# A spectral layer and an attention convolution on one core: the mode loads held behind the row transform, and one pair of transform 1 with 128 stationary columns

## The reference

```python
x = x + _L0_conv_ref(_gn(x), L0_conv_weight, L0_conv_fc_w, L0_conv_fc_b)
x = x + _L1_conv_ref(_gn(x), L1_conv_dft_weight, L1_conv_ksm_w, L1_conv_bias, L1_conv_fbm_scale)
```

```python
x_ft = jnp.fft.rfftn(x, axes=(-2, -1))
blk = jnp.einsum('bimn,hiomn->bhomn', x_ft[:, :, :m1, :m2], w_c)      # 32 x 32 modes
...
xr = jnp.fft.irfftn(out_ft, s=(H, W), axes=(-2, -1))
return jnp.einsum('bchw,oc->bohw', xr, fc_w) + fc_b[None, :, None, None]
```

## Time and profile before

| | |
|---|---|
| median of 3 runs | 139.55 us (138.25 to 139.67) |
| the profiled execution | 139.57 us, of it the span 137.8 us |
| busy: PE, DVE, ACT, POOL | 122.5, 87.8, 70.7, 52.8 us |
| TensorE's granted clock | 0.995 of full speed |
| code packets (queue 8) | 16, 0.26 MB |
| data moved | 25.17 MB, mean 183 GB/s |

### The profile page before, as it was taken

How to read it: one execution, slowest core, us unless ns; L and a number is a source line. 1 busy time by engine, 2 the same in 40 slices (tenths; PEclk the granted TensorE clock), 3 DMA queues, 4 the chain that set the end, 5 groups by cost and what they waited for, 6 DMA issues and landing times.

```text
span 137.8 us, 4822 instructions
## 1 busy us (share of the span) xinstructions
PE 122.5 (89%) x2060; PEld 91.8 (67%) x2060; DVE 87.8 (64%) x201; ACT 70.7 (51%) x143; POOL 52.8 (38%) x44
## 2 busy tenths in 40 slices
PE   0799997969997969979999979989999999999970
PEld 0799997869996959979999969873323432223230
DVE  0077696879996743553357685999873789922340
ACT  0468458538965336523317775644998329311100
POOL 7993000009999999999600550130500000000000
PEclk9999999999999999999999999999999999999997
DMA  3999999999500036787876899887989968884477
GB/s 90 268 272 257 233 222 357 302 384 399 204 5 7 0 81 156 171 203 165 181 164 153 172 178 153 180 202 164 168 184 175 211 156 189 195 191 105 104 162 143
DMA packets 71892, 25.17 MB, mean 183 GB/s; under 512 B 67904, under 2 KB 68160, under 8 KB 71872
## 3 DMA queue, kind: packets, MB, share of 16 engines
q1 hardware_dynamic: 70784, 24.62, 77.2%
q10 hardware_dynamic: 1088, 0.26, 0.9%
HBM read 14.38 MB, written 4.19 MB: 135 GB/s over the span
## 4 chain that ended last, share of the span: by engine, by line
PE 86%; issue 5%; DVE 3%; DMA 2%; ACT 0%; SPq 0%
PE slot L1050 27%; PE slot L882 14%; PE slot L963 11%; PE slot L978 8%; PE slot L941 6%; PE slot L952 5%; PE slot L908 3%; PE aggp L1008 3%; PE slot L904 3%; DMA x_buf<-x 2%; PE small L904 1%; PE aggp L904 1%; DVE kern L780 1%; PE aggp L941 1%; PE small L892 1%
## 5 line engine op out<-in xcount | busy, mean ns | idle before, releaser
L1050 PE MATMUL slot<-y_buf,conv_w 128*32 128x512 f32 (+1 forms) x136 | 31.7, 603 | 0.0
L1050 PE MATMUL slot<-w_buf,conv_w 128*32 128x512 f32 (+1 forms) x136 | 31.7, 603 | 0.0
L882 PE MATMUL slot<-cst,x_buf 128*64 128x64 f32 x512 | 19.0, 241 | 5.3 <-DMA x_buf<-x 4.5
L882 PEld LDWEIGHTS slot<-cst,x_buf 128*64 128x64 f32 x512 | 18.4, 154 | 5.6 <-issue 5.5
L821 DVE TENSOR_TENSOR bd_buf<-slot,q_buf 128x512 f32<-128x512 f32 (+1 forms) x17 | 11.0, 670 | 9.3 <-PE slot L1050 9.1
L1050 PEld LDWEIGHTS slot<-y_buf,conv_w 128*32 128x32 f32 x136 | 8.3, 109 | 12.6 <-issue 12.0
L441 POOL TENSOR_TENSOR x_buf<-y_buf 128x1024 f32<-128x1024 f32 x4 | 7.7, 1934 | 22.5 <-DVE y_buf L709 22.5
L978 PE MATMUL slot<-cst,t_buf 128*128 128x128 f32 x128 | 15.5, 278 | 0.8 <-issue 0.8
L978 PEld LDWEIGHTS slot<-cst,t_buf 128*128 128x128 f32 x128 | 14.7, 192 | 1.4 <-issue 1.2
L963 PE MATMUL slot<-cst,r_buf 128*64 128x128 f32 x256 | 14.6, 274 | 0.7 <-ACT r_buf L491 0.7
L613 DVE TENSOR_REDUCE row_sq<-q_buf 128x16 f32<-128x1024 f32 (+1 forms) x9 | 9.8, 1097 | 7.7 <-ACT q_buf L459 7.7
(11 more groups left out here) (128 smaller groups left out, 222.7 us busy)
## 6 DMA issues: line engine op xcount, KB each, us to landing
x_buf<-x SPq DMA_DIRECT2D x16, 256.0 KB, 4.3
w_buf<-w_modes SPq DMA_DIRECT2D x16, 256.0 KB, 5.0
x_buf<-x SPq DMA_DIRECT2D x32, 128.0 KB, 3.1
w_buf<-y_buf SPq DMA_DIRECT2D x16, 256.0 KB, 5.9
out<-bd_buf SPq DMA_DIRECT2D x28, 128.0 KB, 2.8
t_buf<-dft_w SPq DMA_DIRECT2D x4, 288.0 KB, 5.3
t_buf<-x_buf SPq DMA_DIRECT2D x8, 128.0 KB, 2.4
r_buf<-x_buf SPq DMA_DIRECT2D x8, 128.0 KB, 3.4
```

Of the source, the lines that this page charges most:

```text
L882: last = pe.matmul(ps[64 * ri:64 * ri + 64, col:col + 64], x_part(k)[:, i, q, :], const("fwd_h")[:, 64 * ri:64 * ri + 64], start=True, sto ...
L1050: last = pe.matmul(ps[32 * j:32 * j + 32, 32 * u0:32 * u1], cw[r][:, b, k, :], src, start=(k == terms[0][0]), stop=(k == terms[-1][0]))
```

## The change

There are two edits. SyncE waits until `f1_done` has reached 14 before it issues the first mode load. And in `f2_part` the pair (k, s) = (1, 3), that is images 6 and 7 of part 1 in both groups, takes the form with one matmul of 128 stationary columns for an image in place of two with 64; what is computed stays the same.

```diff
--- before.py
+++ after.py
@@ -318,6 +318,7 @@
                     load_rows(sp, k, q)
                 if k == 1:
                     sp.dma_start(cst[:, 128:EPS1 + 1], consts[:, 128:EPS1 + 1]).then_inc(fwd_w_in, 16)
+            sp.wait_ge(f1_done, 14)
             for ml in range(4):
                 for q in range(4):
                     sp.dma_start(modes[:, ml, 8 * q:8 * q + 8].rearrange("p n xo -> p (n xo)"), w_modes[ml, q]
@@ -900,7 +901,7 @@
                 ml = 4 * xx + k
                 for b in (2 * s, 2 * s + 1):
                     col, f = 64 * b, 4 * ml
-                    if k >= 2:
+                    if k >= 2 or (k, s) == (1, 3):
                         last = pe.matmul(ps[:, col:col + 64], y_rows[:, b, f:f + 4, :].rearrange("w g c -> w (g c)"),
                                          const("fwd_w")[:, 0:64], start=True, stop=True)
                         continue
```

## The result

The changed kernel takes 140.57 us in the median of 10 runs (139.64 to 142.72), the kernel before 139.42 in 10 (138.25 to 140.60): ratio 1.010, 95% interval 1.006 to 1.014. Forecast were 140.0 us and no difference beyond 1%; measured is one at that border, on the slow side.

What follows compares the result with a forecast made beforehand. PE bounds the kernel, busy 122.5 of 137.8 us, with 3.94 us of waits for code. Early gaps removed, a new gap covering 0.40 us of extra work: net +0.4, plus 1.77 around the span, 140.0 us; range 137.9 to 141.9.

Steps and rivals of the forecast that it cites:

- Code packets wait behind the data issued before them: PE's code blocks: each packet waits for all data issued before its request; PE's four gaps total 3.94 us.
- Part 1: SyncE's wait before the mode loads: gaps of 0.72 and 1.22 us go, 0.5 of the first counted; delayed loads stay hidden.
- The new gap in the second product: Second mode product: code packet starts at 38.1, ready at 40.7, wanted at 38.9; PE waits 1.8 us.
- Part 2: Pair (1, 3) with 128 columns: 0.40 us more on PE, covered by the wait in the second mode product.
- The shift by eight records: Later block boundaries move 8 records on; 0.8 us of work slips under the last gap, near the full-width product.
- this sign of being right: Last gap should stand some six records into the full-width product, whose sixth record comes at 52.2 against 51.75.
- The sum: Up to the full-width product's sixth record: 52.2 against 51.75, so 0.4 us slower, giving 140.0 us.
- From there two more follow in today's rhythm: After the block ready at 44.5 against 43.24, two more take 7.7 us as before; sixth full-width record at 52.2.
- (a): Packet for the second mode product isn't held up, starts at 35.55, PE never waits for it: 137.5 us; chance 0.18.
- (b): Packet for the second mode product stands behind all held loads and starts at 41.0: 142.9 us; chance 0.14.
- (c): PE's unexplained gaps are not code and stay, with 0.40 us added for the 128 columns: 140.0 us; chance 0.08.
- (d): First two gaps stay because image loads alone delay the packets; wait ends 0.5 us later: 140.5 us; chance 0.07.

Runs made afterwards that it cites:

- small loads first: Changed kernel with kernel weights, parameters and late constants issued before SyncE's wait, only the modes behind it; 0.997 and 0.999 of the kernel before.
- hold to 12: Changed kernel with SyncE waiting for 12 of 16 halves of the row transform in place of 14; 140.27 us, ratio 1.001 to the kernel before.
- hold alone: Changed kernel with pair (1, 3) back at two matmuls of 64 columns, SyncE's wait kept; 141.53 us, ratio 1.010 to the kernel before.
- hold to 16: Changed kernel with SyncE waiting for all 16 halves of the row transform in place of 14; 141.84 us, ratio 1.013 to the kernel before.
- split hold: Changed kernel with SyncE's wait for 14 halves placed behind the first four mode loads; 140.25 us, ratio 1.006 to the kernel before.
- 128 columns alone: Changed kernel without SyncE's wait, the 128-column form kept, measured twice; 138.64 and 140.03 us, ratios 1.002 and 1.000 to the kernel before.
- first profile: Profiled execution of the changed kernel from the first time it was measured, the fastest of its ten; 139.64 us.
- pacing: Changed kernel without SyncE's wait, at most four mode loads outstanding instead, 128 columns kept; 141.41 us, ratio 1.008 to the kernel before.
- second measurement: Changed kernel, nothing altered, timed again in 12 executions; 140.65 us against 139.87 for the kernel before, ratio 1.004.
- first measurement: Changed kernel as first timed, 10 executions; 140.57 us against 139.42 for the kernel before, ratio 1.010.
- third measurement: Changed kernel, nothing altered, timed once more in six executions; 142.16 us against 140.00 for the kernel before, ratio 1.020.
- short hold: Changed kernel with SyncE's wait for 14 halves placed behind the sixth mode load; 140.32 us, ratio 1.005 to the kernel before.

## Why the prediction was right, and where it was not

**Code packets wait behind the data issued before them: right, and shown.** The starts forecast were 20.2, 24.0, 38.1 and 41.9; they were 20.2, 23.8, 37.7 and 41.7. Volumes moved at the delayed packet against volumes issued: 9.03 to between 8.96 and 9.25 in the changed kernel, 10.15 of 10.19 with the small loads first, 10.11 of 10.19 with the hold to 12. The match is within some 0.2 MB, not exact. In the six profiles in which SyncE was still issuing (the changed kernel's three, hold alone, hold to 16, split hold) the volume moved, 8.3 to 9.8 MB, is what SyncE had issued 0.4 to 0.8 us before the mode products began, an estimate from its issue times. With the 128 columns alone the packet started at 36.6, with 10.05 of 10.19 MB moved, and there is no gap in the second product.

**Part 1, the release and what hides: right in the first profile.** Release 23.1 (forecast 23.6), gaps of 0.72 and 1.22 gone. The pairs began at 26.8 (27.2), 0.9 us earlier than before, where I had counted 0.5. But this part isn't shown to be the hold's: the 128 columns alone, without a hold, had no gap near 22.8 either and began the pairs at the same 26.81. The second gap is absent in all six profiles with the hold to 14 ahead of all mode loads; of the three without any hold or pacing, two have it (1.22 and 0.63 us) and one doesn't. No product waited for its modes in any profile of the changed kernel. The new gap in the second product: 1.59 us (1.8).

**Part 2: size right, 0.42 us (0.40),** measured between two uninterrupted stretches, and covered by the new gap, as said. The equal cost that the prediction worked out from the Trainium skill ("TensorE: Matmul & The Clock Gate", section LDWEIGHTS) doesn't hold for this form: 4.61/40 = 0.115 us a record against 2.48/80 = 0.031. The shift by eight records does what was said: the last gap leaves the end of the mode products. With the 128 columns alone, the second time, 0.12 us of it stand exactly six records into the full-width product. In the changed kernel's profiles nothing of it is left there, so this sign of being right failed to appear.

**The sum: close, and with two things missing.** In the first profile the full-width product came 0.16 us later than before, where the forecast had 0.4: its sixth record at 51.33 + 5 x 0.116 = 51.9 instead of 52.2. The step "From there two more follow in today's rhythm" is the one that didn't hold. From the end of the third gap to the full-width product passed 51.33 - 44.37 = 6.96 us, before 51.17 - 43.24 = 7.93, and what ended last was no longer code but the copies of the last mode product, 0.62 us of waiting that the sum doesn't have.

The other thing missing is PE's clock. The sum was made for 2.4 GHz throughout. It says of the new gap only that PE waits; that PE can come back at 1.2 GHz stands nowhere in it. Of the fourteen profiles, the five without a fall are of executions of 137.8 to 140.1 us, the four with a short one of 139.6 to 140.9, the four with a long one of 141.9 to 142.8, and the one with both took 144.0. The mean clock of every execution tells how much of the loss this is:

| median us (executions) | changed | before, beside it |
|---|---|---|
| second measurement, no fall | 140.05 (3) | 139.77 (27) |
| second, clock 0.98 to 0.99 | 140.52 (6) | 139.89 (5) |
| second, clock below 0.98 | 142.24 (3) | 141.44 (3) |
| third, clock below 0.98 | 142.23 (5) | 141.41 (7) |

Like beside like, the changed kernel is 0.3 to 0.8 us slower; in its first measurement the four executions without a fall took 139.95 to 140.41 us, near the 140.0 of the forecast. The counts are small. The rest of the loss is how often the clock falls: in 21 of 28 executions, against 22 of 82. So the kernel before has falls as well, and a long one costs it 1.7 to 2.0 us (141.44 against 139.77, and in the third measurement 141.41 against 139.40). That the forecast of no difference beyond 1% came out is in part luck: the first measurement lies at its border, the second inside, and the third, where all six executions had a fall, outside.

**The rivals.** (a) The packet not held up: out, it started at 37.7. (b) Behind all of the loads: out for the changed kernel, whose packet started with 9.03 of 10.19 MB moved. The place is that of the small loads first and of the hold to 12, but with the packet at 37.8 and 38.6, not at 41, since the loads then end earlier too. (c) The gaps are not code: out, by the volumes, and by the last gap, which left the mode products with Part 2 and came back without it. (d) The first two gaps stay: out in the first profile; a first gap of 0.45 us was there in the third, and its absence in the first isn't shown to be the hold's.

What stays open is when the clock falls, and why the hold makes it fall more often; that its gap in the second product does so is argued from the four falls that begin at that gap's end. With the small loads first it fell in one profile (gaps of 0.27 and 2.11 us) and not in the other (1.10 and 1.69). Nor was a version found that beats the kernel before: the 128 columns alone and the small loads first are level with it.

## What to carry to other kernels

This long unrolled program loads its own code while it runs, in packets that queue behind the data issued before. In another one of this kind, count records between unexplained "issue" gaps, look for the instruction packets, and compare the volume moved at their start with the volume issued. Holding loads back to clear the way at one block moved them in front of another, so put the bytes where PE's records are slow (0.116 us each), and have the queues empty where they are fast (0.018). And a stall inside a dense stretch of matmuls can have a second price, the clock behind it, which depends on what follows: price it from a stretch at 1.2 GHz, and count over all executions how often it is paid, since one profile shows only one.

## What the runs showed of the hardware

The granted clock fell to 1.2 GHz behind PE gaps as short as 1.5 to 2.3 us in an otherwise dense stream: in the first profile PE stood idle from 38.6 to 40.2, and the clock was down from 40.2. It is no rule of the gap's length alone: with the short hold and with the 128 columns alone a single gap of 2.1 and 2.0 us in the third product left the clock where it was. Of the ten falls in nine profiles, four began at the end of the gap in the second product (40.2, 40.4, 41.3 and 41.8 us) and six 0.5 to 1.9 us behind the end of the one in the third (44.2 to 48.6), up to which PE had stood idle for 1.4 to 2.3 us. The kernel before, in whose profile no gap is longer than 1.22 us and the clock stayed up, was below 0.99 in 22 of 82 executions. The Trainium skill ("TensorE: Matmul & The Clock Gate", section A second HAM failure mode: psum-queue depth-cycling) tells of a kernel whose clock swings because PE idles briefly and often between groups of matmuls. These traces are near that but not the same: one fall or two in an execution, each behind a single gap or a pair of gaps. At 1.2 GHz, a record of a mode product took 0.028 us instead of 0.017, one of 128 columns 0.21 instead of 0.116.
